# Second attention of a mixed transformer kernel: the Newton steps of the layer norm moved from VectorE to GpSimd

## What is computed

```python
def _layernorm(x, axis=-1, eps=1e-05):
    m = jnp.mean(x, axis=axis, keepdims=True)
    v = jnp.var(x, axis=axis, keepdims=True)
    return (x - m) / jnp.sqrt(v + eps)
...
x = x + attn_a(_layernorm(x))
x = x + ffn(_layernorm(x))      # 16 experts, top 2, a capacity for each expert
x = x + attn_b(_layernorm(x))   # 16 heads of 8; the top 6 queries by their largest score attend
x = x + ffn(_layernorm(x))
```

## Time and profile before

| | |
|---|---|
| median of 3 runs | 1549.39 us (1541.33, 1549.39, 1552.91) |
| profiled execution | 1551.83 us, of which the span is 1549.5 us |
| mean granted TensorE clock | 0.891 |
| second attention's score records (L1814) | 562.8 to 1272.9 us from the span's start |

### The profile page before, as it was taken

The page is one execution under the profiler, slowest core; times in us unless marked ns, Lnnn a source line. Parts: engine busy times, 40 slices in busy tenths (PEclk is TensorE's granted clock), DMA queues, the critical chain, the costliest instruction groups (busy, mean ns, idle before and its releaser), DMA issues.

```text
span 1549.5 us, 28769 instructions
## 1 busy us (share of the span) xinstructions
PE 1305.2 (84%) x8534; PEld 802.8 (52%) x8534; DVE 1137.9 (73%) x5084; ACT 768.2 (50%) x1903; POOL 732.2 (47%) x1041
## 2 busy tenths in 40 slices
PE   3988888887899999999999999999999989999300
PEld 1555554454798964444444444444444448888300
DVE  3898998898473658788888889888888784755422
ACT  2343443341564766555655656556555556646200
POOL 2135555446423213354555655545554342347775
PEclk9999999999899988888988979978888889999755
DMA  6645412001354520000000000110000003557522
GB/s 171 226 140 176 139 57 75 27 24 55 112 187 155 176 83 14 10 19 26 22 23 28 29 21 21 38 60 28 29 25 18 28 29 121 162 159 229 161 80 70
DMA packets 119770, 125.82 MB, mean 81 GB/s; under 512 B 15552, under 2 KB 109888, under 8 KB 119616
## 3 DMA queue, kind: packets, MB, share of 16 engines
q1 hardware_dynamic: 103232, 90.42, 18.2%
q0 software_dynamic: 16384, 33.59, 7.5%
HBM read 50.15 MB, written 73.79 MB: 80 GB/s over the span
## 4 chain that ended last, share of the span: by engine, by line
PE 49%; DVE 27%; issue 7%; POOL 7%; ACT 5%; DMA 3%; SPq 1%; POOLq 0%; ACTq 0%; DVEq 0%
PE pair L1814 19%; DVE pT L1321 7%; PE pair L1741 7%; POOL vmyg L522 5%; DVE pT L1047 3%; PE pair L1752 3%; DVE xs L1231 3%; PE pair L1730 2%; PE pair L1605 2%; ACT pT L816 2%; PE bank L1544 2%; PE bank L1550 2%; PE bank L1842 2%; DVE st L898 2%; PE bank L1802 1%
## 5 line engine op out<-in xcount | busy, mean ns | idle before, releaser
L1814 PE MATMUL pair<-kT,apart 32*128 32x512 f32 x2048 | 480.6, 743 | 34.7 <-DVE smax L1321 33.4
L816 ACT ACTIVATE pT<-pair 128x256 f32<-128x256 f32 x1024 | 328.9, 396 | 259.0 <-PE pair L1814 257.5
L1321 DVE CUSTOM_DVE_ANT_0 pT<-pair,pT 128x256 f32<-128x256 f32 x1024 | 381.4, 417 | 100.9 <-ACT pT L816 97.4
L1814 PEld LDWEIGHTS pair<-kT,apart 32*128 32x128 f32 x2048 | 196.0, 210 | 194.7 <-DVE smax L1321 118.9
L1741 PE MATMUL pair<-xeT,unit_w 128*128 128x256 f32 x768 | 186.9, 387 | 0.0
L1047 DVE TENSOR_TENSOR pT<-pair,causal 128x512 f32<-128x512 f32 x256 | 158.4, 680 | 23.8 <-PE pair L1605 23.8
L522 POOL DMA_INDIRECT vmyg<-ybufA,slg x128 | 122.3, 955 | 84.9 <-issue 36.6
L1206 DVE TENSOR_TENSOR hid<-sg,pair 128x512 f32<-128x512 f32 x96 | 65.9, 686 | 126.3 <-ACT sg L742 125.9
L1741 PEld LDWEIGHTS pair<-xeT,unit_w 128*128 128x128 f32 x768 | 142.0, 195 | 16.0
L482 POOL DMA_INDIRECT dispB<-xnf,sli x128 | 126.5, 988 | 43.6 <-issue 43.6
L482 POOL DMA_INDIRECT dispA<-xnf,sli x128 | 126.9, 992 | 40.6 <-issue 40.6
(11 more groups left out here) (235 smaller groups left out, 2025.8 us busy)
## 6 DMA issues: line engine op xcount, KB each, us to landing
dispB<-zeros SPq DMA_DIRECT2D x16, 1408.0 KB
apart<-dispA SPq DMA_DIRECT2D x96, 128.0 KB
ybufA<-ye SPq DMA_DIRECT2D x48, 256.0 KB
apart<-dispB SPq DMA_DIRECT2D x96, 128.0 KB
ybufB<-ye SPq DMA_DIRECT2D x48, 256.0 KB
dispA<-zeros SPq DMA_DIRECT2D x33, 128.0 KB
xs<-in_x SPq DMA_DIRECT2D x16, 256.0 KB, 3.0
out<-xs SPq DMA_DIRECT2D x16, 256.0 KB, 2.5
```

What stands on the lines that cost most here:

```text
L816: act.activation(rel[n % RING][:, q, :], pair[n % RING][:, q, HALF:SEQ], ACT.Relu).then_inc(s["relu_done"], 1)
L1321: dve.tensor_tensor_reduce(out=rel[n % RING][:, q, :], in0=pair[n % RING][:, q, 0:HALF], in1=rel[n % RING][:, q, :], scale=1.0, scalar=LOW ...
L1814: pe.matmul(pair[n % RING][:, q, :], apart[h][at, j, t * P:(t + 1) * P], kTs[h][at, HALF:], start=True, stop=True).then_inc(s["bsc_done"], 1)
```

## The change

In the second attention the three Newton steps are no longer made by VectorE behind pairs 30, 31 and 0. GpSimd makes them in its own body, behind the sends and the wait for their landing, and ahead of the two norms. A step on GpSimd has four operations (VectorE's fused last one becomes an addition and a multiplication), so there are 12 of them, each behind a wait on the one before. `row_shift` is gone: GpSimd's norm now subtracts the mean and multiplies by rstd, where it multiplied by rstd and added nmr. VectorE keeps the statistics, the aggregates and the first guess. Since GpSimd reads the mean now, VectorE waits for the norms of the seam before, ahead of its aggregates. Single norms outside of the batches (the first two and the last) keep VectorE's steps, and GpSimd's new form of the norm serves them too. The list of semaphore names gets `rs_pool`.

```diff
@@ -242,6 +242,10 @@
                  "idx_done idc_done sel_done qsel_done qsel_ready att_done amax_done aneg_done aexp_done aeT_done aeT_ready cx_done cx_ready "
                  "cw_done ainv_done cw_ready bo_done x_out settled xnf_free fetched")
         s = {n: sem(n) for n in names.split()}
+
+        def rs_before(call):
+
+            return 11 * min(call, CALLS + 2) + 2 * max(call - CALLS - 2, 0)
 
         block = ctx.enter_context(nc.Block())
 
@@ -606,11 +610,28 @@
 
                 pool.wait_ge(s["rstd_ready"], call + 1)
                 at = slice(q * TB, q * TB + TB)
-                pool.tensor_tensor(dst[:, :, :], xs[:, tiles_of(b), :], rstd[:, at].unsqueeze(2).to_broadcast([P, TB, D]),
-                                   ALU.mult).then_inc(s[kind + "_scaled"], 1)
+                pool.tensor_tensor(dst[:, :, :], xs[:, tiles_of(b), :], mv[:, at, 0:1].to_broadcast([P, TB, D]),
+                                   ALU.subtract).then_inc(s[kind + "_scaled"], 1)
                 pool.wait_ge(s[kind + "_scaled"], n - B + 1)
-                pool.tensor_tensor(dst[:, :, :], dst[:, :, :], nmr[:, at].unsqueeze(2).to_broadcast([P, TB, D]),
-                                   ALU.add).then_inc(s[kind + "_xn_ready"], 1)
+                pool.tensor_tensor(dst[:, :, :], dst[:, :, :], rstd[:, at].unsqueeze(2).to_broadcast([P, TB, D]),
+                                   ALU.mult).then_inc(s[kind + "_xn_ready"], 1)
+
+            def newton(call, W):
+
+                at = 11 * (call - CALLS - 2)
+                pool.wait_ge(s["rs"], rs_before(call) + 2)
+                for r in range(3):
+                    y, z = lny[r % 2], (lny[1 - r % 2] if r < 2 else rstd)
+                    if r:
+                        pool.wait_ge(s["rs_pool"], at + 4 * r)
+                    pool.tensor_tensor(lnt[:, 0:W], y[:, 0:W], y[:, 0:W], ALU.mult).then_inc(s["rs_pool"], 1)
+                    pool.wait_ge(s["rs_pool"], at + 4 * r + 1)
+                    pool.tensor_tensor(lnu[:, 0:W], lnt[:, 0:W], lnh[:, 0:W], ALU.mult).then_inc(s["rs_pool"], 1)
+                    pool.wait_ge(s["rs_pool"], at + 4 * r + 2)
+                    pool.tensor_scalar(lnt[:, 0:W], lnu[:, 0:W], 1.5, None, ALU.add).then_inc(s["rs_pool"], 1)
+                    pool.wait_ge(s["rs_pool"], at + 4 * r + 3)
+                    last = pool.tensor_tensor(z[:, 0:W], lnt[:, 0:W], y[:, 0:W], ALU.mult)
+                    last.then_inc(s["rs_pool" if r < 2 else "rstd_ready"], 1)
 
             def body(b, u, h, x, last=True, next=True, fetch_=True, before=True):
                 if not next:
@@ -629,6 +650,7 @@
                     places(b - 2, b - 2 + B, h)
                     send(b - 2 + B, u - 1 + B // 2, h)
                     sent(u - 1 + B // 2, h)
+                newton(b + 2 + CALLS, TB * (last + fetch_))
                 if last:
                     normed(b - 1, b - 1 + B, xnf[1 - h], "ffn", 0, b + 2 + CALLS)
                 if fetch_:
@@ -905,6 +927,10 @@
 
             def row_aggregates(call, W):
                 dve.wait_ge(s["stats"], call + 1)
+                if call > CALLS:
+
+                    dve.wait_ge(s["att_xn_ready"], min(call - CALLS + B, 2 * B))
+                    dve.wait_ge(s["ffn_xn_ready"], call - CALLS + B - 3)
                 for j in range(W):
                     last = dve.bn_aggr(mv[:, j, :], st[:, j, :])
                 last.then_inc(s["moments"], 1)
@@ -918,23 +944,23 @@
 
                 dve.tensor_scalar(lnv[:, 0:W], mv[:, 0:W, 1], EPS, None, ALU.add).then_inc(s["rs"], 1)
                 dve.tensor_scalar(lnh[:, 0:W], mv[:, 0:W, 1], EPS, -0.5, ALU.add, ALU.mult)
-                dve.wait_ge(s["rs"], call * 11 + 1)
+                dve.wait_ge(s["rs"], rs_before(call) + 1)
                 dve.tensor_scalar(lny[0][:, 0:W].bitcast(I32), lnv[:, 0:W].bitcast(I32), -0.5, float(0x5f3759df),
                                   ALU.mult, ALU.add).then_inc(s["rs"], 1)
 
             def newton(call, W, steps):
                 for r in steps:
                     y, z = lny[r % 2], (lny[1 - r % 2] if r < 2 else rstd)
-                    dve.wait_ge(s["rs"], call * 11 + 2 + 3 * r)
+                    dve.wait_ge(s["rs"], rs_before(call) + 2 + 3 * r)
                     dve.tensor_tensor(lnt[:, 0:W], y[:, 0:W], y[:, 0:W], ALU.mult).then_inc(s["rs"], 1)
-                    dve.wait_ge(s["rs"], call * 11 + 3 + 3 * r)
+                    dve.wait_ge(s["rs"], rs_before(call) + 3 + 3 * r)
                     dve.tensor_tensor(lnu[:, 0:W], lnt[:, 0:W], lnh[:, 0:W], ALU.mult).then_inc(s["rs"], 1)
-                    dve.wait_ge(s["rs"], call * 11 + 4 + 3 * r)
+                    dve.wait_ge(s["rs"], rs_before(call) + 4 + 3 * r)
                     dve.scalar_tensor_tensor(out=z[:, 0:W], in0=lnu[:, 0:W], scalar=1.5, in1=y[:, 0:W],
                                              op0=ALU.add, op1=ALU.mult).then_inc(s["rs"], 1)
 
             def row_shift(call, W):
-                dve.wait_ge(s["rs"], call * 11 + 11)
+                dve.wait_ge(s["rs"], rs_before(call) + 11)
                 dve.scalar_tensor_tensor(out=nmr[:, 0:W], in0=mv[:, 0:W, 0], scalar=-1.0, in1=rstd[:, 0:W],
                                          op0=ALU.mult, op1=ALU.mult).then_inc(s["rstd_ready"], 1)
 
@@ -1376,8 +1402,6 @@
             def body(b, u, h, x, last=True, next=True, fetch=True, before=True):
                 for n in range(PAIRS):
                     largest(b, h, n)
-                    if last and n == 0:
-                        last_newton(b - 1)
                     if fetch and n == 1:
                         indices(b + 2, h)
                     if b == MID + 1 and n == 30:
@@ -1427,22 +1451,9 @@
                         if last:
                             row_aggregates(call, TB)
                         first_guess(call, norm_width(b))
-                    if n in (30, 31):
-                        newton(b + 2 + CALLS, norm_width(b), (n - 30,))
-                if not next:
-                    last_newton(b)
 
             def norm_width(b):
                 return TB * ((b > 0) + (b + 2 < B))
-
-            def last_newton(b):
-
-                if b + 1 < B:
-                    dve.wait_ge(s["att_xn_ready"], min(b + B + 2, 2 * B))
-                if b > 1:
-                    dve.wait_ge(s["ffn_xn_ready"], b + B - 1)
-                newton(b + 2 + CALLS, norm_width(b), (2,))
-                row_shift(b + 2 + CALLS, norm_width(b))
 
             def fetched_stats(b, second):
 
@@ -1457,6 +1468,8 @@
             def fetched_aggregates(b):
 
                 q = TB * (b > 0)
+                dve.wait_ge(s["att_xn_ready"], b + B + 2)
+                dve.wait_ge(s["ffn_xn_ready"], b + B - 1)
                 if b:
                     dve.wait_ge(s["stats2"], b)
                 else:
```

More of the change, by code:

```diff
@@ L231, in build @@
         bank = [pb(f"bank{i}") for i in range(2)] + [pair[i // 2][:, i % 2, :] for i in range(2 * RING)]
-        names = ("w_in w_in2 vm_zero consts1 consts2 consts3 headof_done qbias_done ms0 ms1 wnr x_in0 x_in1 bias_added " + " ".join(f"{k}_{n}" for k in ("att", "ffn") for n in "xn_ready tp_done xT_ready".split()) + " stats moments rs rstd_ready "
+        names = ("w_in w_in2 vm_zero consts1 consts2 consts3 headof_done qbias_done ms0 ms1 wnr x_in0 x_in1 bias_added " + " ".join(f"{k}_{n}" for k in ("att", "ffn") for n in "xn_ready tp_done xT_ready".split()) + " stats moments rs rs_pool rstd_ready "
                  ""
```

## The result

The changed kernel takes 1594.22 us (median of 4 runs, 1592.24 to 1597.22), the kernel before 1545.36 us in the runs beside it. The ratio is 1.033, with a 95% interval of 1.025 to 1.041: slower. 1587 us was forecast, in a range of 1556 to 1615. A second measurement on another occasion gave 1585.96 against 1546.84 us, ratio 1.028 (1.023 to 1.033). The profiled execution took 1597.22 us, of which 1595.1 us are the span. Ratios leave out executions more than 1.5% above the fastest of the same kernel.

What follows compares the result with a forecast made beforehand. No engine is full, so the order of waits decides, at the seam between batches. Stalls 29.3 - 3 given back + 11 clock = 37.3 us on the profiled 1551.8 gives 1589.1, or 1587 us from the median; range 1556 to 1615.

Steps and rivals of the forecast that it cites:

- The price of the steps: GpSimd, between the sends' landing and the norms: 12 dependent operations take 3.8 us per batch, bounds 1.9 to 4.8.
- GpSimd's chain as a floor: From `keep` to the `xnf` transposes, every batch takes at least 19.8 us, however early TensorE comes.
- The sum of the stalls: TensorE at the `xnf` transposes: new stall of 3.8 us less the slack in each of 13 seams, 29.3 us together.
- The removal at zero: VectorE in the seam: losing 1.9 us per batch gains nothing, as TensorE runs gapless there; at most 30 us.
- The clock: TensorE behind the stalls: low clock after idle time costs 11 us, bounds 0 and 44.
- 3 given back: Four fast seams, behind the transposes: the stall lets VectorE catch up, returning 4 x 0.7 = 3 us.
- The fast one: Seam: VectorE is the true bound and GpSimd's steps take only 1.9 us; 1519 or 1526 us, chance 0.07.
- The second: GpSimd's steps take 1.9 to 2.5 us, most seams absorb them, clock takes nothing; 1553 to 1564 us, chance 0.15.
- The third: Stalls as summed, but each seam brings two low-clock stretches, 44 us; 1622 us, chance 0.10.
- The covers: Behind the first norm: second norm adds no stall; gathers start 3.8 us later, covered by 10 us key waits.

Runs made afterwards that it cites:

- one operation: Changed kernel with GpSimd's 12 Newton operations cut to one that copies the first guess into rstd; 1533.6 us, ratio 0.991 to the kernel before.
- split order: Changed kernel with GpSimd making six sends, Newton steps, both norms, then two sends and their wait; 1525.76 us, ratio 0.985 to the kernel before.
- VectorE's load kept: Changed kernel with ten useless VectorE operations on scratch tiles in the removed places; 1589.76 us, against 1585.96 us for the changed kernel beside it.
- the ring that goes on: Changed kernel in split order, its score-buffer ring index running on across batches instead of restarting; 1518.07 us, ratio 0.981 to the kernel before.

## Why the prediction was right, step by step

- *The price of the steps.* I took 3.8 us between two readings of dependent starts, 4.2 and 3.5. It is 3.48. The reading from the big norm pair (the next starts 0.08 us after the end) was the right one. By reported durations alone it would have been 2.5.
- *GpSimd's chain as a floor.* Forecast 19.8 us from `keep` to the transposes; in the seam shown it is 794.32 - 774.55 = 19.8. That every seam becomes equally long is seen in the trace.
- *The sum of the stalls.* Forecast 29.3 us more from rank to transposes, measured 25.3. The steps were 0.3 us shorter, in 12 seams 4 us. TensorE's waits themselves sum to 35.0 us, more than forecast, since it comes to the transposes earlier: its rows of 16 records are 5.8 us shorter, which I had put at nothing. The floor set by GpSimd took that back.
- *The removal at zero.* This step failed when taken by itself: with GpSimd in time, or nearly, the relief is worth 13 us (one operation, GpSimd late in four seams) to 21 us (split order). The row that I read, 4.64 us, happened to be one of the shortest of the 13. In the changed kernel the relief is hidden behind the stall, as the variant with VectorE's load kept shows, so the sum was not harmed.
- *The clock.* Forecast 11 us less 3 given back = 8 us; from transposes to the next rank it was 20.8 us in the profiled execution. In this trace the term was mis-sized, by 13 us, and it has two halves. I had 22 us more at the low level (one stretch of 3.4 us in half of the seams), and there were 88. I charged half of that time as lost, and 20.8 of 88 us is a quarter. In the second trace there were 58 us more at the low level and 9 us lost, close to the forecast. So the term has no one size; it stood within my bound of 44 both times. That the idle stretch brings the low clock was only partly right: 18 us come back when TensorE is kept busy in the stall, but the clock also falls without such a stretch (the ring that goes on), and in three seams of the variant with one operation it stays high behind 1.47 us of idle time.
- *The rivals.* The fast one fell with the sign; its claim on VectorE was worth about half of its price (13 to 21 us of 30). The second needed steps of at most 2.5 us, and they took 3.48. The third needed 44 us from the clock, and there were 21 and 9.
- *The covers.* The gathers stand behind the longer chain, and VectorE's idle time ahead of its additions didn't grow (79.0 us in the page, 81.8 before); the second norm adds no stall (the transposes at 799.08 in this seam follow without idle time).

The span grew by 45.6 us where 37.3 were forecast: the stalls 4 us under, the clock 13 us over. In the second measurement the profiled span is 31.3 us above that of before. That the failed step was hidden is luck in the number, not in the sign. So is part of how near 1587 us came, since executions of the changed kernel differ by about as much as the terms erred: they go from 1582 to 1597 us.

## What to carry to other kernels

When work is moved to an engine with idle time, look at the slack ahead of the one instruction that waits for its result, not at its busy share: here 47% busy, and 0.2 to 2.1 us of slack in 12 of 13 seams. Place such work under a wait that exists anyway: the same twelve operations and the norms, moved up by two sends and the wait for the landing, turned 3.3% slower into 1.5% faster. And judge a gapless TensorE by how long the same records take in other batches at the same granted clock, since a busy row can hold a wait, and a longer one can also be a slower clock.

## What the runs showed of the hardware

Dependent GpSimd operations of 128x8 start 0.29 us apart though each reports 0.20 to 0.23 us. The same row of 16 score records took 3.43, 4.38 and 5.33 us at a mean granted clock of 1.00, 0.67 and 0.50, and at 0.67 another 0.6 us where VectorE was behind. 1.45 us less of GpSimd's chain in 13 seams took some 40 us away, and two useless matmuls in a stall made a kernel 18 us faster without less time at the low clock in its trace; it lay ahead of the transposes and not behind them. The clock fell after idle stretches of 1.47 us in most seams, not in all, and once the stretch was gone it fell there all the same.
